# Two blocks of a short convolution as diagonal products on TensorE, gate half last, in a two-layer decoder kernel

## The reference, cut to what matters

```python
for i in range(nl):                                   # 4 layers
    h = _rms(x, norm_w[i])
    xz = jnp.einsum('bld,ed->ble', h, W_in[i])        # 256 -> 2 x 512
    xi, z = jnp.split(xz, 2, axis=-1)
    xp = jnp.pad(xi, ((0, 0), (dc - 1, 0), (0, 0)))
    xc = conv_b[i] + sum((xp[:, k:k + L, :] * conv_w[i][:, k] for k in range(dc)))   # dc = 4
    xc = _silu(xc)
    dbc = jnp.einsum('bld,ed->ble', xc, W_x[i])       # 512 -> 64 + 16 + 16
    delta, Bm, Cm = jnp.split(dbc, [rk, rk + n], axis=-1)
    delta = softplus(jnp.einsum('blr,dr->bld', delta, W_dt[i]) + b_dt[i])
    deltaA = jnp.exp(delta[..., None] * A)            # A = -exp(A_log), 16 states
    BX = (delta * xc)[..., None] * Bm[:, :, None, :]
    hs = scan(deltaA, BX)                             # along time
    y = jnp.einsum('bldn,bln->bld', hs, Cm) + D[i] * xc
    x = x + jnp.einsum('bld,ed->ble', y * _silu(z), W_out[i])
```

## Time and profile before

| what | us |
|---|---|
| median of 3 runs | 1365.56 |
| the three runs | 1355.98, 1365.56, 1367.28 |
| the profiled execution | 1356.69 |
| its span (first to last instruction) | 1354.9 |
| the state space block, first scan to last gate product | 365.6 to 1073.8 |
| mean granted TensorE clock | 0.937 |

### The profile page before, as it was taken

The page is one execution under the profiler, slowest core; times in us unless marked ns, Lnnn a source line. Parts: engine busy times, 40 slices in busy tenths (PEclk is TensorE's granted clock), DMA queues, the critical chain, the costliest instruction groups (busy, mean ns, idle before and its releaser), DMA issues.

```text
span 1354.9 us, 17349 instructions
## 1 busy us (share of the span) xinstructions
PE 1126.2 (83%) x5914; PEld 653.0 (48%) x5914; DVE 1099.4 (81%) x1644; ACT 794.7 (59%) x1758; POOL 849.8 (63%) x751
## 2 busy tenths in 40 slices
PE   7798888878488898988988889889896988888874
PEld 3455555544144553544545435455453555555544
DVE  3577777565599999999999999999998858776656
ACT  1555555565267567666776666756743355556654
POOL 6001111100599899998999999999999534445405
PEclk9899999989789899998999989989998999999975
DMA  6000001000501504106032060140410210000000
GB/s 201 12 12 12 12 12 70 1 1 3 222 10 45 193 1 170 42 1 238 0 114 97 1 237 0 53 158 0 171 55 0 53 44 16 17 31 2 1 1 25
DMA packets 22140, 79.12 MB, mean 58 GB/s; under 512 B 4935, under 2 KB 8847, under 8 KB 21138
## 3 DMA queue, kind: packets, MB, share of 16 engines
q1 hardware_dynamic: 22054, 78.02, 16.5%
HBM read 76.77 MB, written 1.24 MB: 58 GB/s over the span
## 4 chain that ended last, share of the span: by engine, by line
POOL 34%; PE 31%; DVE 21%; ACT 7%; issue 6%; DMA 1%; SPq 0%; ACTq 0%; DVEq 0%; POOLq 0%
PE ps L627 28%; POOL arena L1779 20%; POOL arena L1791 11%; DVE ps L1864 5%; DVE hstat L1081 4%; ACT arena L862 2%; PE ps L698 2%; DVE arena L1869 2%; DVE arena L1867 2%; DVE arena L1829 2%; ACT arena L872 1%; DMA arena<-in_exb 1%; ACT L622 1%; DVE arena L1069 1%; POOL arena L1768 1%
## 5 line engine op out<-in xcount | busy, mean ns | idle before, releaser
L627 PE MATMUL ps<-arena 128*32 128x100 f32 (+10 forms) x3188 | 474.7, 375 | 55.3 <-ACT arena L862 25.6
L627 PE MATMUL ps<-arena,ident 128*128 128x400 f32 x1024 | 395.7, 538 | 100.9 <-POOL arena L1791 65.9
L1779 POOL TENSOR_TENSOR arena<-arena 128x1600 f32<-128x1600 f32 x128 | 456.8, 3582 | 21.6 <-DVE arena L1132 12.1
L1679 ACT ACTIVATE ps<-arena 128x400 f32<-128x400 f32 x512 | 283.0, 589 | 180.0 <-DVE arena L1867 132.0
L627 PEld LDWEIGHTS ps<-arena 128*32 128x32 f32 (+9 forms) x3188 | 242.0, 144 | 248.3 <-issue 113.5
L627 PEld LDWEIGHTS ps<-arena,ident 128*128 128x128 f32 x1024 | 201.1, 202 | 281.1 <-issue 68.3
L1864 DVE TENSOR_TENSOR_SCAN ps<-ps,arena 128x800 f32<-128x800 f32 x160 | 291.2, 1820 | 15.1 <-ACT ps L1679 8.6
L862 ACT ACTIVATE arena<-ps,hstat 100x361 f32<-100x361 f32 x256 | 143.8, 564 | 106.0 <-DVE hstat L1081 105.8
L601 POOL TENSOR_SCALAR stat<-stat 100x1 f32<-100x1 f32 (+1 forms) x44 | 8.7, 198 | 293.3 <-DVE stat L582 291.9
L1791 POOL TENSOR_TENSOR arena<-arena 128x1600 f32<-128x1600 f32 x48 | 171.7, 3576 | 17.2 <-DVE arena L1869 17.2
L1869 DVE TENSOR_TENSOR_SCAN arena<-ps,arena 128x800 f32<-128x800 f32 x96 | 168.7, 1806 | 7.3 <-POOL arena L1779 4.7
(11 more groups left out here) (187 smaller groups left out, 1038.6 us busy)
## 6 DMA issues: line engine op xcount, KB each, us to landing
arena<-bc_scratch SPq DMA_DIRECT2D x64, 800.0 KB, 6.7
arena<-in_ctxT SPq DMA_DIRECT2D x16, 361.0 KB, 3.8
arena<-in_w_in SPq DMA_DIRECT2D x4, 1024.0 KB, 6.3
arena<-in_expT SPq DMA_DIRECT2D x1, 2048.0 KB, 12.4
arena<-in_w_out SPq DMA_DIRECT2D x4, 512.0 KB, 3.2
arena<-in_mask SPq DMA_DIRECT2D x8, 141.0 KB
arena<-in_xT SPq DMA_DIRECT2D x2, 400.0 KB, 4.3
x_tok<-in_x_tok SPq DMA_DIRECT2D x1, 800.0 KB
```

Source lines behind the costliest of these rows:

```text
L627: return nc.tensor.matmul(outp, lhsT, rhs, start=first, stop=last)
L1679: last = nc.scalar.activation(psf[:, half_at(k) + j * GT:half_at(k) + (j + 1) * GT], delta[g][:, c], ACT.Exp, scale=aneg[:, l % 2, n:n + 1])
L1779: nc.gpsimd.tensor_tensor(bx[:, unit % BX].rearrange("p (j t) -> p j t", j=SEGMENT), bbc[:, nq].rearrange("p (j t) -> p j t", j=SEGMENT), ...
```

## The change

Blocks 2 and 3 of the convolution leave DVE. PE makes X2 and X3 first; ACT copies them raw to SBUF (`am_raw_x`, u = 7); PE makes Y2 and Y3 from the copies, each as four products with a diagonal matrix of one tap, over 400, 396, 392 and 388 columns, accumulated in PSUM (`pm_conv`, u = 8); ACT adds the bias on the way out (`am_conv_out`, u = 8). The diagonal matrices are made by ACT from the identity, four of 128 x 128 for each block, once a layer (`am_taps`, u = 5 and 6 of round 0 and of rounds 1, 3, 5). Blocks 0 and 1 keep the old way: PE u = 9, ACT u = 9, DVE u = 10.

The gate half X4 to X7 is made last, at u = 15 and 16 (that is, u = 0 of the next round), copied by ACT at the same units, and activated at u = 3 of the round that uses it, between two table loads of its own. The SiLU of xc at u = 11 is cut into two of 800 columns (blocks 2, 3, then 0, 1), and `pm_dbc` starts with blocks 2, 3; it stands at u = 11 on PE, and D0, D1 at u = 12. ACT's copy of dbc stays at u = 12, its softplus steps at u = 13 and 14. Unit 8 joins `DVE_C`: its product with C goes from POOL to DVE. ACT's diagonal of D (`am_skip`, rounds 0, 2, 4, 6) goes from u = 3 to u = 2. `dx` has one buffer in place of two, so `gm_delta` waits for the last B product that read the block; the queue SP loads the next layer's weights after X6, X7 were copied, where before it was after D2, D3.

```diff
-DVE_C = (0, 3, 4, 5, 7, 10, 11, 13, 14, 15)
+DVE_C = (0, 3, 4, 5, 7, 8, 10, 11, 13, 14, 15)
...
-    "aK": 3,
+    "aK": 2,
     "aQ": 4,
     "gN": 4,
     "aH": 5,
     "pT": 7,
     "aT": 6,
-    "pX": (9, 9, 11, 11, 8, 8, 8, 8),
-    "aC": (9, 9, 10, 10),
-    "vC": (9, 10),
-    "aZ": (7, 7, 8, 8),
+    "pX": (9, 9, 8, 8, 15, 15, 16, 16),
+    "aG": (5, 6),
+    "aX": 7,
+    "aY": 8,
+    "aC": 9,
+    "vC": 10,
+    "aZ": (15, 15, 16, 16),
+    "aV": 3,
     "aS": 11,
-    "pB": 12,
+    "pB": 11,
     "aB": 12,
-    "pD": (13, 13, 14, 14),
+    "pD": (12, 12, 14, 14),
...
+        taps = mam.take(2, DC, P)
+        mam.at += CD * GT - 2 * DC * P
+        dx = mam.take(CD, GT)
...
-        IN_ORDER = [*range(CD, 2 * CD), *range(CD)]
-        PREP = ["T0", "T1"] + [f"X{e}" for e in IN_ORDER] + ["DB"] + [f"D{c}" for c in range(CD)]
+        PREP = (["T0", "T1", "X2", "X3", "Y2", "Y3", "X0", "X1", "DB"] + [f"D{c}" for c in range(CD)]
+                + [f"X{e}" for e in range(CD, 2 * CD)])
...
+        def pm_conv(pe, m, c):
+
+            pe.wait_ge(m_taps, m // G + 1)
+            n = f"Y{c}"
+            p_read(pe, m, f"X{c}")
+            p_free(pe, m, n)
+            y3 = ps[:, p_bank(m, n), 0:GT].rearrange("p (b t) -> p b t", b=GB)
+            x3 = xc[m % G][:, c].rearrange("p (b t) -> p b t", b=GB)
+            for s in range(DC):
+                last = mm(y3[:, :, s:S], taps[:, c - 2, DC - 1 - s], x3[:, :, 0:S - s], s == 0, s == DC - 1)
+            last.then_inc(m_full, 1)
+
         def pm_dbc(pe, m):
-            pe.wait_ge(m_xc, m + 1)
             p_free(pe, m, "DB")
-            for c in range(CD):
-                last = mm(ps[0:RK + 2 * NS, p_bank(m, "DB"), 0:GT], w_x[:, c, :], xc[m % G][:, c], c == 0, c == CD - 1)
+            for k, c in enumerate((2, 3, 0, 1)):
+                if k % 2 == 0:
+                    pe.wait_ge(m_xc, 2 * m + k // 2 + 1)
+                last = mm(ps[0:RK + 2 * NS, p_bank(m, "DB"), 0:GT], w_x[:, c, :], xc[m % G][:, c], k == 0, k == CD - 1)
...
+        def am_raw_x(act, m, g, c):
+
+            n = f"X{c}"
+            p_full(act, m, n)
+            nc.scalar.activation(xc[g][:, c], ps[:, p_bank(m, n), 0:GT], ACT.Copy).then_inc(p_done(m, n), 1)
+
+        def am_conv_out(act, m, g, c):
+
+            n = f"Y{c}"
+            p_full(act, m, n)
+            nc.scalar.activation(xc[g][:, c], ps[:, p_bank(m, n), 0:GT], ACT.Identity, bias=cvb[:, c:c + 1],
+                                 scale=1.0).then_inc(p_done(m, n), 1)
+
+        def am_taps(act, m, l, c):
+
+            act.wait_ge(ld_w, 80 * (l + 1))
+            if m and c == 2:
+                p_full(act, m, "Y3")
+            for k in range(DC):
+                last = nc.scalar.activation(taps[:, c - 2, k], ident[:, :], ACT.Identity,
+                                            scale=cvw[:, DC * c + k:DC * c + k + 1])
+            if c == 3:
+                last.then_inc(m_taps, 1)
...
+            for names, c in ((("Y2", "Y3"), 2), (("X0", "X1"), 0)):
+                for n in names:
+                    p_read(act, m, n)
+                nc.scalar.activation(xc[g][:, c:c + 2], xc[g][:, c:c + 2], ACT.Silu).then_inc(m_xc, 1)
+
+        def am_silu_z(act, m, g):
+            if m:
                 for c in range(CD):
-                    p_read(act, m, f"X{c}")
-            nc.scalar.activation(xc[g][:, :], xc[g][:, :], ACT.Silu).then_inc(m_xc, 1)
+                    p_read(act, m, f"X{CD + c}")
             nc.scalar.activation(sz[g][:, :], sz[g][:, :], ACT.Silu).then_inc(m_sz, 1)
...
+                    for c in range(CD):
+                        if m and u == AT["aZ"][c] - UNITS:
+                            am_z(act, m, g, c)
+                    if m and u == AT["aV"]:
+                        table(act, SET_SILU)
+                        am_silu_z(act, m, g)
+                        table(act, SET_EXP_LN)
...
+                    for c in (2, 3):
+                        if u == AT["aG"][c - 2] and (m == 0 or g == 1):
+                            am_taps(act, m, l + g, c)
+                        if u == AT["aX"]:
+                            am_raw_x(act, m + 1, ng, c)
+                    for c in (2, 3):
+                        if u == AT["aY"]:
+                            am_conv_out(act, m + 1, ng, c)
+                    for c in range(2):
+                        if u == AT["aC"]:
+                            am_conv(act, m + 1, ng, c)
...
+                pool.wait_ge(m_bx, UNITS * (m - 1) + NQ * (c + 1))
+            nc.gpsimd.tensor_tensor(dx[:, c], delta[g][:, c], xc[g][:, c], ALU.mult).then_inc(m_dx, 1)
...
-                        for k in range(2):
-                            if u == AT["vC"][k]:
-                                vm_conv(dve, m + 1, ng, 2 * k)
+                        if u == AT["vC"]:
+                            vm_conv(dve, m + 1, ng, 0)
```

More of the change, by code:

```diff
@@ L287, in decoder @@
         bbc, cbc = mam.take(NQ, SEGMENT * GT), mam.take(NQ, SEGMENT * GT)
-        delta, dx, xc, sz = [None, None], [None, None], [None, None], [None, None]
-        delta[1], dx[1], dx[0] = (mam.take(CD, GT) for _ in range(3))
+        delta, xc, sz = [None, None], [None, None], [None, None]
+        delta[1] = mam.take(CD, GT)
+        taps = mam.take(2, DC, P)
+        mam.at += CD * GT - 2 * DC * P
+        dx = mam.take(CD, GT)
         bx = mam.take(BX, SEGMENT * GT)
@@ L1374, in mam_sync @@
                 if g == 1 and l + 1 < NL:
-                    p_read(sp, m, "D2")
-                    p_read(sp, m, "D3")
+                    p_read(sp, m, "X6")
+                    p_read(sp, m, "X7")
                     sp_weights(sp, l + 1)
@@ L1393, in pm_in @@
         def pm_in(pe, m, e):
-            if e == CD:
+            if e == (2 if m else CD):
                 pe.wait_ge(ld_w, 80 * (m // G + 1))
@@ L1506, in mam_pe @@
                 for u in range(UNITS):
+                    for e in range(CD, 2 * CD):
+                        if m and u == AT["pX"][e] - UNITS:
+                            pm_in(pe, m, e)
                     if m and u == AT["pO"]:
@@ L1514, in mam_pe @@
                             pm_turn(pe, m + 1)
-                        for e in range(2 * CD):
+                        if u == AT["pX"][2]:
+                            for c in (2, 3):
+                                pm_in(pe, m + 1, c)
+                            for c in (2, 3):
+                                pm_conv(pe, m + 1, c)
+                        for e in (0, 1, *range(CD, 2 * CD)):
                             if u == AT["pX"][e]:
@@ L1549, in am_raw @@
             p_full(act, 0, n)
-            nc.scalar.activation(dx[0][:, c], ps[:, p_bank(0, n), 0:GT], ACT.Copy).then_inc(p_done(0, n), 1)
+            nc.scalar.activation(dx[:, c], ps[:, p_bank(0, n), 0:GT], ACT.Copy).then_inc(p_done(0, n), 1)
         def am_tap(act, c):
             p_read(act, 0, f"X{c}")
-            nc.scalar.activation(xc[0][:, c], dx[0][:, c], ACT.Identity, bias=cvb[:, c:c + 1],
+            nc.scalar.activation(xc[0][:, c], dx[:, c], ACT.Identity, bias=cvb[:, c:c + 1],
                                  scale=cvw[:, DC * c + DC - 1:DC * c + DC]).then_inc(m_acc, 1)
@@ L1628, in am_silu @@
                     p_read(act, 0, f"X{CD + c}")
-            else:
+                nc.scalar.activation(xc[g][:, :], xc[g][:, :], ACT.Silu).then_inc(m_xc, 2)
+                am_silu_z(act, 0, 0)
+                return
+            for names, c in ((("Y2", "Y3"), 2), (("X0", "X1"), 0)):
[4 more added lines that the diff above has]
+            if m:
                 for c in range(CD):
-                    p_read(act, m, f"X{c}")
-            nc.scalar.activation(xc[g][:, :], xc[g][:, :], ACT.Silu).then_inc(m_xc, 1)
+                    p_read(act, m, f"X{CD + c}")
             nc.scalar.activation(sz[g][:, :], sz[g][:, :], ACT.Silu).then_inc(m_sz, 1)
@@ L1706, in mam_act @@
                             am_z(act, m + 1, ng, c)
-                    for c in range(CD):
-                        if u == AT["aC"][c]:
-                            am_conv(act, m + 1, ng, c)
                     if u == AT["aS"]:
@@ L1767, in gm_delta @@
                 p_read(pool, m, f"D{c}")
-            nc.gpsimd.tensor_tensor(dx[g][:, c], delta[g][:, c], xc[g][:, c], ALU.mult).then_inc(m_dx, 1)
+                pool.wait_ge(m_bx, UNITS * (m - 1) + NQ * (c + 1))
+            nc.gpsimd.tensor_tensor(dx[:, c], delta[g][:, c], xc[g][:, c], ALU.mult).then_inc(m_dx, 1)
             pool.wait_ge(m_dx, CD * m + c + 1)
```

7 lines of the change are left out of this document (4 added, 3 removed).

## The result

The changed kernel takes 1347.13 us in the median of 16 runs (1343.18 to 1356.79), the kernel before 1356.95 us in 16 runs of the same sessions (1350.5 to 1367.28). The ratio is 0.9935, with a 95% interval of 0.9913 to 0.9958: 8.8 us less by the ratio. A second series gave 1348.16 us, ratio 0.9945 (0.992 to 0.9969). The forecast was 6.9 us less, and 1354.5 as a time. The time was set against 1361.4, the mean of the four executions known then; the 16 runs of the kernel before fill the space from 1350.5 to 1367.28 rather than two places, and their median is 4.4 us lower.

The account below looks back on a forecast made before the run. DVE sets the pace (84.3 us busy of 86.7 to 89.2 a round), POOL a hair behind. Terms -9.6 - 7.6 - 4.1 + 5.2 + 5.7 + 3.5 = -6.9 us, against the mean of 1361.4: 1354.5, range 1335 to 1371.

Parts of the forecast that it names:

- within 1%: Whole execution between 1348 and 1375 us, neither faster nor slower by over 1%; chance 0.58.
- Less DVE work, -9.6: DVE: six fewer tap steps in seven rounds, 24.1 us less; unit 8's product 14.5 more; together -9.6.
- the late X1: PE's X1 arriving as unit 10's exponentials fall due; priced at 0 to 0.8 us a round, taken as 0.
- Two waits gone, -7.6: DVE's waits for POOL ahead of unit 9 (0.57) and ACT's first tap (0.51) go: 7.6 us less.
- Half of the falls gone, -4.1: TensorE clock falls at the round's end: half of 8.2 us goes, -4.1, bounds 0 and -8.2.
- The gate's SiLU, +5.7: ACT's loads and SiLU at u = 3 delay unit 4 by 0.95 us, six times: +5.7, from 3 to 8.
- The tap matrices, +5.2: ACT at u = 5 and 6 of four rounds: 1.3 us each, +5.2, bounds 2 and 7.
- PE's order at the round's end, +3.5: Gate blocks behind D3 delay the last sum for DVE's gate product 0.5 us a round: +3.5, from 0 to 8.
- the drain: Rival: a pause before each of two more ACT table loads in seven rounds, 18 us, time 1372; chance 0.02.
- The falls: Rival: clock falls every round between dbc and D3, 3.2 us a round, 22.4 in seven, 1373; chance 0.13.
- the freed time is waited again at unit 15: Rival: ACT's chain through softplus to unit 15 sets the pace, nothing is left, 1361; chance 0.12.

Follow-up runs that it names:

- the first profile: The changed kernel, unedited, in its first profiled execution, against the kernel before: block from first scan to last gate product 693.3 us, where before 708.2.
- the second: The changed kernel profiled again with no edit: block 698.9 us, ratio 0.9945 against the kernel before.
- experiment 1: The changed kernel with unit 8's C product back on POOL: block 694.1 us, ratio 0.9888 against the kernel before.
- experiment 12: The kernel before with three spare products a round on PE at u = 14: block 701.6 us, ratio 0.9943.
- experiment 4: The changed kernel, gate's SiLU at u = 3 of rounds 1 to 7 replaced by a copy, without its two table loads: block 689.8 us, ratio 0.9892.

## Why the prediction was right, point by point

The forecast was 6.9 us less with a range of 1335 to 1371 and 0.58 on "within 1%"; the ratio of 0.9935 is 8.8 us less. The mechanism was the one described: the places of the new waits and the removal of the old ones came as listed. That the sum came so near is in part luck. Entries were off both ways, and the block of the first profile is 15.0 us shorter, that of the second 9.4. In us over the block, from the first profile:

- **Less DVE work, -9.6.** Busy time in the block 671.9 to 665.0, -6.9; with the last round's product, hidden there by POOL as said (its waits there are 2.41 in place of 1.02 and 3.38), that is -9.0. Right as a sum. As prices of the two parts it was wrong: the product was put at 2.07 a round and the late X1 at 0, and experiment 1 shows that without the product the late X1 costs 1.74 to 1.93 a round. The step that failed is that the two were taken as independent: 14.5 us looked like a price that undoing the product would give back, and the block gives next to nothing back.
- **Two waits gone, -7.6.** Both gone in all seven rounds; they were 7.3 in sum. Right.
- **Half of the falls gone, -4.1.** Before, the falls hold 9.2 us above the waits of a clean round, 7.2 ahead of unit 15 in five rounds and 2.0 at two gate products; experiment 12 takes 6.7 off the block and leaves two of the waits. In the first profile of the changed kernel the falls hold 1.9 (0.5 in each of four rounds, ahead of unit 15), in the second 8.2 (three rounds with 2.2 and three with 0.5). So the entry is -7.3 in one execution and -1.0 in the other. That their mean is -4.1 is luck; the half was a guess, and which rounds are hit isn't predictable from one profile.
- **The gate's SiLU, +5.7.** 0.88 to 1.04 in each round, 5.8 in the six that were counted, and gone without the loads (experiment 4). Right in size and place.
- **The tap matrices, +5.2.** 0.65 in three rounds, and in round 0 1.39 against 0.23 before: 3.1. The place was right, the size too large. The delay carried over from the first set was put at 0.6 and is nothing: the second set starts 1.75 us after DVE starts on unit 6 (rows below), and before, ACT was at the same place 1.85 us after the earlier trace rows, since its wait of 0.64 us for DVE ahead of the second exponentials took the first set in. What is left is 1.17 of the second set less 0.48 of room, 0.69. There was no wait at unit 6.
- **PE's order at the round's end, +3.5.** 0.27 or 0.28 in three rounds, 0.8. Too large, and within the bounds of 0 and 8.

```profile
484.01 3.54 DVE L1946 TENSOR_TENSOR_SCAN arena<-ps,arena 128x800 f32<-128x800 f32 x2
...
485.76 1.30 ACT L1666 ACTIVATE arena<-ident,arena 128x128 f32<-128x128 f32 x4
```

With 1.1 us less in what else changed in the last round these entries add up to the 15.0 of the first profile. Without the clock they come to -7.7, where the forecast had -2.8; the taps and PE's order are most of that difference.

Of the rivals, the drain did not come. The falls did, at the place that was named: at the sum behind D0 and D1 in four rounds of the first profile and six of the second, and at dbc in two rounds and one. Their price did not: 1.9 and 8.2 us in all, where the rival had 22.4. It had taken the price of a fall, 2.71, from the dearest of five; DVE's wait in the other four rounds before was 1.39 to 1.42. That the freed time is waited again at unit 15 did not come. In experiment 1 freed time of DVE is waited again wholly, but ahead of unit 10 and for another cause.

What stays open: what decides whether the clock falls behind a gap. The same kernel does both behind 2.22 us, and the changed one behind 1.86, and no run here was made to tell. Nor was the last round's 2.41 us of wait for POOL tried.
